# Low-rank factors split into 16-bit halves before the feed-forward weights are merged, in a perceiver block on one core

## The reference

```python
x = x + fake_quant(layernorm(x)) @ fake_quant(ctx)               # ctx: (16, 1024, 1024)
x = x + attention(layernorm(x), qkv_w, qkv_b, out_w, out_b)      # 32 heads of 32, rotary, causal
x = x + ffn(layernorm(x))
# ffn(h):  h @ W.T + bias + sum_e coeffs[e]*scales[e] * (h @ A[e].T) @ Bf[e].T     A: (16, 16, 1024)
```

## Time and profile before

| | us |
|---|---|
| median of 3 runs | 678.24 (678.01 to 678.92) |
| the profiled execution: its own time | 679.87 |
| its span (first to last record of the core) | 678.2 |
| TensorE's matmuls, busy | 619.1 (91%) |
| VectorE, busy | 457.4 (67%) |
| ScalarE, busy | 293.8 (43%) |

### The profile page before, as it was taken

The page is one execution under the profiler, slowest core; times in us unless marked ns, Lnnn a source line. Parts: engine busy times, 40 slices in busy tenths (PEclk is TensorE's granted clock), DMA queues, the critical chain, the costliest instruction groups (busy, mean ns, idle before and its releaser), DMA issues.

```text
span 678.2 us, 12785 instructions
## 1 busy us (share of the span) xinstructions
PE 619.1 (91%) x4848; PEld 311.2 (46%) x4848; DVE 457.4 (67%) x931; ACT 293.8 (43%) x370; POOL 7.6 (1%) x18
## 2 busy tenths in 40 slices
PE   0648967689999999999999999999999999799998
PEld 0223533345555554555555455555544544344453
DVE  8698984846854884586398558747754467675861
ACT  3986657256346346525643553555201233111010
POOL 1100000000000000000000000000000000000000
PEclk9869987879999999999999999999999999999999
DMA  8999864374157308514740761274300061032221
GB/s 321 388 387 401 303 257 155 104 254 147 58 186 242 130 17 295 182 62 146 249 162 0 275 220 62 103 268 154 125 31 1 1 238 75 1 108 95 92 83 57
DMA packets 38329, 109.09 MB, mean 161 GB/s; under 512 B 3994, under 2 KB 4250, under 8 KB 38304
## 3 DMA queue, kind: packets, MB, share of 16 engines
q1 hardware_dynamic: 36528, 104.35, 43.2%
q0 software_dynamic: 1344, 4.23, 1.6%
q10 hardware_dynamic: 432, 0.18, 0.1%
HBM read 100.35 MB, written 8.39 MB: 160 GB/s over the span
## 4 chain that ended last, share of the span: by engine, by line
PE 79%; DVE 14%; issue 3%; ACT 2%; DMA 1%; DVEq 0%; SPq 0%; ACTq 0%
PE dense L1032 14%; PE dense L1034 14%; PE dense L1033 14%; PE cross L1054 7%; PE turn L1022 6%; PE dense L1148 4%; PE cross L1174 4%; PE dense L1150 4%; PE dense L1149 4%; PE score L1109 3%; PE score L1135 2%; DVE wq L714 2%; PE dense L1041 1%; PE score L1098 1%; DVE nw L657 1%
## 5 line engine op out<-in xcount | busy, mean ns | idle before, releaser
L1032 PE MATMUL dense<-wq,xn_h 128*128 128x512 f16 x448 | 172.1, 384 | 5.1 <-DVE wq L782 2.3
L1033 PE MATMUL dense<-wq,xn_h 128*128 128x512 f16 x448 | 171.6, 383 | 0.0
L1034 PE MATMUL dense<-wq,xn_l 128*128 128x512 f16 x448 | 171.6, 383 | 0.0
L294 ACT ACTIVATE code<-raw,cst,qc 128x1024 uint8<-128x1024 f32 x77 | 94.4, 1238 | 16.8 <-DMA raw<-in_ctx 16.4
L1054 PE MATMUL cross<-code,q1t 128*128 128x512 f16 x256 | 76.0, 401 | 15.7 <-DVE xa L723 9.9
L1034 PEld LDWEIGHTS dense<-wq,xn_l 128*128 128x128 f16 x448 | 44.2, 99 | 54.2 <-issue 2.2
L1032 PEld LDWEIGHTS dense<-wq,xn_h 128*128 128x128 f16 x448 | 44.2, 99 | 53.7 <-issue 8.4
L1033 PEld LDWEIGHTS dense<-wq,xn_h 128*128 128x128 f16 x448 | 44.2, 99 | 46.4 <-issue 4.8
L745 DVE TENSOR_REDUCE smx<-score 128x8 f32<-128x512 f32 x32 | 21.9, 685 | 53.9 <-PE score L1109 53.9
L310 ACT ACTIVATE at<-turn 128x512 f32<-128x512 f32 x32 | 19.1, 596 | 87.1 <-PE turn L1022 87.1
L733 DVE TENSOR_TENSOR rope<-dense,cst 128x512 f32<-128x512 f32 x32 | 22.0, 688 | 49.4 <-PE dense L1034 49.4
(11 more groups left out here) (128 smaller groups left out, 852.6 us busy)
## 6 DMA issues: line engine op xcount, KB each, us to landing
raw<-in_ctx SPq DMA_DIRECT2D x77, 512.0 KB, 4.6
lnt<-in_ctx SPq DMA_DIRECT2D x35, 512.0 KB, 4.0
wq<-in_qkv_w SPq DMA_DIRECT2D x11, 512.0 KB, 13.4
wo<-in_qkv_w SPq DMA_DIRECT2D x10, 512.0 KB, 11.5
wo<-in_ctx SPq DMA_DIRECT2D x8, 512.0 KB, 8.6
wq<-in_ctx SPq DMA_DIRECT2D x8, 512.0 KB, 11.7
x_scratch<-xb SPq DMA_DIRECT2D x8, 512.0 KB, 3.0
wq<-x_scratch SPq DMA_DIRECT2D x8, 512.0 KB, 3.6
```

The source lines that it names most:

```text
L294: act.activation(low_bytes, src, ACT.Identity, scale=qc[:, 1:2], bias=z2).then_inc(s_u8, 1)
L1032: pe.matmul(bank[:, :], a_h[:, k, :], w_hi, start=(k == 0 and not started), stop=False)
L1033: pe.matmul(bank[:, :], a_h[:, k, :], w_lo, start=False, stop=False)
L1034: ins = pe.matmul(bank[:, :], a_l[:, k, :], w_hi, start=False, stop=(k == KC - 1))
```

## The change

The factors are no longer used as float32. SyncE loads each of the four pieces (128 x 1024: two of `A2`, two of `B2`) into a staging place of its own: the two halves of `raw`, `q1t`, and `lnt` after the last pair's `x_turn` (`s_xt`). ScalarE makes the high half of each (`lora_high`, times 64, and for `B2` times `w` too), VectorE the low half (`lora_low`). A merge is then six float16 matmuls, the same three terms as in `dense` for each of the two pieces of the rank. The product is 64 x 64 times too large, and `merged_sum` scales it back in the addition that it did already, now a `scalar_tensor_tensor`.

The loads of `W` move: units 0 to 3 into `raw` when two low halves are there (`s_llo` 2), units 4 and 5 into `lnt` when all four are, units 6 and 7 and then the right half after the last `qkv`. TensorE does merges 4 and 5 within `qkv` 5, after the second scores, merges 6 and 7 between the halves of `project`, 8 to 11 behind `y_turn(0)`, and 12 to 15 after rounds 0 to 3 of `ffn(0, 0, 0)`. `y_turn(1)` comes after round 4 instead of 3 of `ffn(0, 0, 1)`.

```diff
@@ views
-        la = code[:, 0:4, :].rearrange("p j d -> p (j d)").bitcast(F32).rearrange("p (j d) -> p j d", j=2)
-        lb = [q1v.bitcast(F32), code[:, 4:6, :].rearrange("p j d -> p (j d)").bitcast(F32)]
+        la = [[code[:, 2 * j + h, :] for h in range(2)] for j in range(2)]
+        lb = [[code[:, 4 + h, :] for h in range(2)], [code[:, 6 + h, :] for h in range(2)]]
+        lora_stage = [raw[:, 0, :], raw[:, 1, :], q1v.bitcast(F32), lnt[:, :]]
+        wt_lnt = lnt[:, :].rearrange("p (u n) -> p u n", u=2)
+        wt_load = {0: 0, 4: 1, 6: 2, 8: 3, 12: 4}
@@ ScalarE
+            def lora_high(n):
+                act.wait_ge(s_lora[n], 16)
+                if n == 0:
+                    act.wait_ge(s_cmm, CHUNKS * PAIRS)
+                if n == 2:
+                    act.wait_ge(s_lws, 1)
+                act.activation(lora_parts(n)[0], lora_stage[n], ACT.Copy,
+                               scale=WSC if n < 2 else lw[:, n - 2, 0:1]).then_inc(s_lhi, 1)
             def last_pair(i):
+                for n in range(4):
+                    lora_high(n)
                 qk_evac(i, 0)
@@ SyncE, after the last context load
-            load_quarter(0)
+            for j in range(2):
+                sp.dma_start(lora_stage[j], lora_a[j * P:(j + 1) * P, :]).then_inc(s_lora[j], 16)
+            sp.dma_start(lw[:, :, :], lora_w.rearrange("(j p) c -> p j c", p=P)).then_inc(s_lw, 16)
             sp.wait_ge(s_cmm, CHUNKS * PAIRS)
-            sp.dma_start(la, lora_a.rearrange("(j p) d -> p j d", p=P)).then_inc(s_ld2, 16)
-            for j in range(2):
-                sp.dma_start(lb[j], lora_b[j * P:(j + 1) * P, :]).then_inc(s_ld2, 16)
-            sp.dma_start(lw[:, :, :], lora_w.rearrange("(j p) c -> p j c", p=P)).then_inc(s_ld2, 16)
+            sp.dma_start(lora_stage[2], lora_b[0:P, :]).then_inc(s_lora[2], 16)
+            sp.wait_ge(s_xt, 2 * PAIRS)
+            sp.dma_start(lora_stage[3], lora_b[P:2 * P, :]).then_inc(s_lora[3], 16)
             store_x2(PAIRS - 2)
+            sp.wait_ge(s_llo, 2)
+            load_wt(0)
+            sp.wait_ge(s_llo, 4)
+            load_wt(1)
             sp.wait_ge(s_qkv, 6 * PAIRS)
-            load_quarter(1)
+            load_wt(2)
             sp.wait_ge(s_st, 32)
-            sp.dma_start(xs[0], x2_dram[0, :, :]).then_inc(s_x2[0], 16)
-            load_quarter(2)
-            sp.dma_start(xs[1], x2_dram[1, :, :]).then_inc(s_x2[1], 16)
-            load_quarter(3)
+            for n in range(2):
+                sp.dma_start(xs[n], x2_dram[n, :, :]).then_inc(s_x2[n], 16)
+            load_wt(3)
+            load_wt(4)
@@ VectorE
             def merged_sum(u):
                 dve.wait_ge(s_wf, u + 1)
-                dve.tensor_tensor(wt_unit(u), X[u % 2][:, :], wt_unit(u), ALU.add).then_inc(s_wsum, 1)
+                dve.scalar_tensor_tensor(wt_unit(u), X[u % 2][:, :], 1.0 / (WSC * WSC), wt_unit(u), ALU.mult, ALU.add).then_inc(s_wsum, 1)
-            def scale_factors():
-                dve.wait_ge(s_ld2, 64)
-                link(dve.tensor_tensor(lw[:, :, 0:1], lw[:, :, 0:1], lw[:, :, 1:2], ALU.mult))
-                for j in range(2):
-                    dve.tensor_scalar(lb[j], lb[j], lw[:, j, 0:1], None, ALU.mult).then_inc(s_lb, 1)
+            def lora_weights():
+                dve.wait_ge(s_lw, 16)
+                dve.scalar_tensor_tensor(lw[:, :, 0:1], lw[:, :, 0:1], WSC, lw[:, :, 1:2], ALU.mult, ALU.mult).then_inc(s_lws, 1)
+                dve.wait_ge(s_lws, 1)
+            def lora_low(n):
+                dve.wait_ge(s_lhi, n + 1)
+                hi, lo = lora_parts(n)
+                dve.scalar_tensor_tensor(lo, lora_stage[n], WSC if n < 2 else lw[:, n - 2, 0:1], hi, ALU.mult, ALU.subtract).then_inc(s_llo, 1)
             def last_pair(i):
-                scale_factors()
+                lora_weights()
+                for n in range(4):
+                    lora_low(n)
                 rotate(i, 0)
...
                 softmax_in(i, 2)
                 softmax_in(i, 3)
+                merged_sum(4)
                 softmax_out(i, 2)
                 softmax_out(i, 3)
+                merged_sum(5)
                 c_low(i, 0)
                 c_low(i, 1)
             def apply3(t, s):
                 if isinstance(t, int) and t == 0:
                     dve.wait_ge(s_xt, 2 * PAIRS)
+                    dve.wait_ge(s_wfl, 6)
@@ VectorE, after the last pair
-            stats3(0, 0)
-            apply3(0, 0)
             for u in range(4):
                 merged_low(u)
-            merged_sum(4)
-            merged_sum(5)
-            out_evac(PAIRS - 1, 0)
+            stats3(0, 0)
             merged_low(4)
             merged_low(5)
-            out_evac(PAIRS - 1, 1)
+            apply3(0, 0)
             merged_sum(6)
-            y_low(0, 0)
             merged_sum(7)
+            out_evac(PAIRS - 1, 0)
             merged_low(6)
             merged_low(7)
+            out_evac(PAIRS - 1, 1)
+            y_low(0, 0)
             merged_sum(8)
             merged(*range(9, 2 * KC))
@@ TensorE
             def merge(u):
                 if u == 0:
-                    pe.wait_ge(s_lb, 2)
+                    pe.wait_ge(s_llo, 4)
                     pe.wait_ge(s_ce, 4 * PAIRS)
                 if u >= 2:
                     pe.wait_ge(s_wsum, u - 1)
+                rank_rows = slice(k * P, (k + 1) * P)
                 for j in range(2):
-                    ins = pe.matmul(X[u % 2][:, :], la[:, j, k * P:(k + 1) * P], lb[j][:, cols],
-                                    start=(j == 0), stop=(j == 1))
+                    pe.matmul(X[u % 2][:, :], la[j][0][:, rank_rows], lb[j][0][:, cols], start=(j == 0), stop=False)
+                    pe.matmul(X[u % 2][:, :], la[j][0][:, rank_rows], lb[j][1][:, cols], start=False, stop=False)
+                    ins = pe.matmul(X[u % 2][:, :], la[j][1][:, rank_rows], lb[j][0][:, cols], start=False, stop=(j == 1))
                 ins.then_inc(s_wf, 1)
-                qkv(i, 5, {0: [at(scores, i, 1)], 1: [at(c, 10, 11)], 2: [at(c, 12, 13)], 3: [at(c, 14, 15), at(values_due, i, 0)], 4: [at(values, i, 0)],
+                qkv(i, 5, {0: [at(scores, i, 1)], 1: [at(c, 10, 11), at(m, 4)], 2: [at(c, 12, 13), at(m, 5)], 3: [at(c, 14, 15), at(values_due, i, 0)], 4: [at(values, i, 0)],
-                    merge(4)
-                    merge(5)
+                    merge(6)
+                    merge(7)
             y_turn(0)
-            for u in range(6, 12):
+            for u in range(8, 12):
                 merge(u)
-                between = {1 + 2 * k: [at(merge, 12 + k)] for k in range(4)} if first and n == 0 else {}
+                between = {k: [at(merge, 12 + k)] for k in range(4)} if first and n == 0 else {}
-                    between = {3: [at(y_turn, 1)]}
+                    between = {4: [at(y_turn, 1)]}
```

More of the change, by code:

```diff
@@ L196, in build @@
         s_st = sem("s_st")
-        s_ld2 = sem("s_ld2")
-        s_wt = [sem(f"s_wt{n}") for n in range(4)]
+        s_lora = [sem(f"s_lora{n}") for n in range(4)]
+        s_lw = sem("s_lw")
+        s_lws = sem("s_lws")
+        s_lhi = sem("s_lhi")
+        s_llo = sem("s_llo")
+        s_wt = [sem(f"s_wt{n}") for n in range(5)]
         s_fb = sem("s_fb")
-        s_lb = sem("s_lb")
         s_wf = sem("s_wf")
@@ L234, in wt_unit, with lora_parts @@
             k, cols = merge_unit(u)
-            return wt_early[:, u, :] if u < 4 else wt[:, k, cols]
+            if u < 4:
+                return wt_early[:, u, :]
+            return wt_lnt[:, u - 4, :] if u < 6 else wt[:, k, cols]
+        wt_load = {0: 0, 4: 1, 6: 2, 8: 3, 12: 4}
+        def lora_parts(n):
+            return la[n] if n < 2 else lb[n - 2]
         def staged(j):
@@ L573, in _, with load_wt @@
             wt_v = ffn_wt.rearrange("(k p) n -> p k n", p=P)
-            def load_quarter(n):
-                ks, cols = slice(4 * (n % 2), 4 * (n % 2) + 4), slice(n // 2 * NT, (n // 2 + 1) * NT)
-                sp.dma_start(wt_early if n == 0 else wt[:, ks, cols], wt_v[:, ks, cols]).then_inc(s_wt[n], 16)
-            load_quarter(0)
+            def load_wt(n):
+                ks = (slice(0, 4), slice(4, 6), slice(6, 8), slice(0, 4), slice(4, 8))[n]
+                cols = slice(0, NT) if n < 3 else slice(NT, DM)
+                sp.dma_start((wt_early, wt_lnt)[n] if n < 2 else wt[:, ks, cols], wt_v[:, ks, cols]).then_inc(s_wt[n], 16)
+            for j in range(2):
+                sp.dma_start(lora_stage[j], lora_a[j * P:(j + 1) * P, :]).then_inc(s_lora[j], 16)
+            sp.dma_start(lw[:, :, :], lora_w.rearrange("(j p) c -> p j c", p=P)).then_inc(s_lw, 16)
             sp.wait_ge(s_cmm, CHUNKS * PAIRS)
-            sp.dma_start(la, lora_a.rearrange("(j p) d -> p j d", p=P)).then_inc(s_ld2, 16)
-            for j in range(2):
-                sp.dma_start(lb[j], lora_b[j * P:(j + 1) * P, :]).then_inc(s_ld2, 16)
```

(24 more changed lines are left out.)

## The result

| | before | changed |
|---|---|---|
| median, us | 678.58 (678.01 to 678.96, 4 runs) | 672.02 (670.29 to 672.18, 4 runs) |
| ratio to before | | 0.9898, 95% interval 0.9880 to 0.9917 |
| profiled execution, us | 679.87, span 678.2 | 670.29, span 668.6 |

The changed kernel is faster by 6.9 us (0.0102 x 678.58; 5.6 to 8.1 by the interval), inside the forecast range of 668.0 to 673.2.

The account below looks back on a forecast made before the run. TensorE was taken as the bound (79% of the chain, VectorE 14%). Terms 6.7 + 1.05 + 2.6 - 2.7 = 7.65 us; with 7.6 off the shown median of 678.24, the forecast was 670.6 us, range 668.0 to 673.2.

Parts of the forecast that it names:

- a merge: On TensorE, six float16 matmuls at 0.216 us, 1.30 us instead of 1.72; 16 merges save 6.7 us.
- factors' split: Ahead of the last pair: rotation 0.3 us late, its consumer `qk_turn(7, 0)` unmoved; priced at 0, at most 1 us.
- wait before the values: TensorE's wait for VectorE's second subtraction in the last pair, filled by merges 4 and 5; 1.05 us gained.
- wait at merge 10: Behind `y_turn(0)`, TensorE stands for VectorE's sum 8; 2.7 us lost, bounds 0 and 3.7 us.
- end of merge 15: Last merge, which sets the next product's time through VectorE; ends at 578.2 against 585.8, 7.6 us sooner.
- next product: TensorE's product after `y_turn(1)`, set by merge 15's end; predicted near 588.9 against 596.56 before.
- The four rounds moved behind the last merge: Merges 12 to 15 after rounds 0 to 3 have four rounds less ahead of them; 2.6 us gained.
- the clock rival: TensorE's clock falls after the new stall; at most 2.9 us, giving 673.5, or 672.1 at half; chance 0.17.
- Less stall: No stall, or half of it, at merge 10; 669.3 to 667.9 us; chance 0.10.
- late VectorE: VectorE later than counted at `apply3(0)` or `c_low`, beyond 0.9 or 1.0 us of slack; about 672 us; chance 0.10.
- unchanged merges: Float16 merges no cheaper on TensorE; only 1.8 us gained, 676.4 us; chance 0.03.
- a blocked merge 0: Merge 0 waits for all four low halves and blocks product 1 of the last pair; slower; chance 0.02.

Follow-up runs that it names:

- mid_no_wait: Changed kernel with merges 4 to 7 all between the halves of the projection and VectorE's order of sum8_early; 0.9861 of the kernel before, stretch 88.19 us.
- high_first: Changed kernel with ScalarE's high halves 6 and 7 ahead of `y_high(0)` instead of behind it; 0.9858 of the kernel before, stretch 88.00 us.
- sum8_early: Changed kernel with VectorE's sums 8 and 9 ahead of low 6 and low 7 and the second output evacuation later; 0.9857 of the kernel before, stretch 86.98 us.
- late_rounds: Changed kernel with merges 12 to 15 back after rounds 1, 3, 5, 7 and `y_turn(1)` after round 3; 0.9927 of the kernel before, stretch 91.98 us.
- f16_old_order: Kernel before with only float16 factors and six-matmul merges, merges and VectorE essentially in the old order; 0.9911 of the kernel before, stretch 91.80 us.
- the second set: The changed kernel, unchanged, timed again against the kernel before; ratio 0.9891 (0.9874 to 0.9908), stretch 89.39 us.
- mid_merges: Changed kernel with merges 4 to 7 all between the halves of the projection, sums 4 and 5 between the first low halves; 0.9925 of the kernel before, stretch 92.30 us.
- longer_wait: Changed kernel with one more 128x1024 addition on VectorE just ahead of sum 8; 0.9926 of the kernel before, stretch 92.19 us.

## Why the prediction was right

The times below count from the start of the stretch, 499.36 before and 497.53 after, so that the early part of the trace stays out.

| step | predicted | measured |
|---|---|---|
| a merge | 1.30 us | 1.30 us |
| factors' split: `qk_turn(7, 0)` | 8.65, unmoved | 506.18 - 497.53 = 8.65 |
| wait before the values | gone, 1.05 | gone; 1.2 with its surroundings, by mid_no_wait |
| `y_turn(0)` | 62.3 | 62.23 |
| wait at merge 10 | 2.70 | 2.56 |
| end of merge 15 | 78.8 | 78.62 |
| `y_turn(1)` | 85.5 | 85.32 |
| next product | 89.5 | 89.39 |
| gain in the stretch | 7.65 | 7.81 |

**Each step.** What the steps add up to was right because the steps were, and not by errors that cancel: the largest is 0.2 us, at merge 15's end. The price of a merge came from rows of the same form and held: 0.216 us a matmul. The figure of the Trainium skill ("TensorE: Matmul & The Clock Gate", section "Back-to-back issue gap"), 131 ns, doesn't fit this stream either, as merges 8 and 9 show at 1.30 us for six. The split costs nothing although VectorE's rotation starts 5.46 us into the stretch (502.99) instead of 5.39: `qk_turn` waits for nothing. The new stall was mis-sized by 0.14 us only; its cause was the queue behind `y_high`, which high_first shows (1.39 us back when high 6 and 7 go ahead) and sum8_early shows from the other side (2.41 us back by order alone). The four rounds moved behind the last merge are worth 2.59 us in late_rounds, against the predicted 2.6.

**The terms weren't additive in one place.** The sum lists 6.7 us for the merges and 2.7 for the stall. f16_old_order shows that cheaper merges in the old order return 5.4, not 6.7: VectorE holds them back there too, by 1.3 us. The new order (merges 4 and 5 early, 12 to 15 early, VectorE's new sequence) adds 2.4 on top, of which 1.2 and 2.6 are gains, each measured in an order of its own, and the rest is paid by the longer wait at merge 10 (2.56 against 1.3 us).

**The whole time.** 670.6 was forecast and 672.02 measured, 1.4 us more. 0.3 of it is the median of the kernel before, which came out at 678.58 and not at 678.24. The change in the times is 6.9 us (or 7.4 in the second set) where the stretch gives 7.8. Both intervals, 5.6 to 8.1 and 6.2 to 8.6, hold 7.8, so there is nothing to explain that the times can tell. The span of 668.6 of the first profile flatters the kernel by the early clock, and the 679.87 us of before was above its median.

**The rivals.** The median of 672.02 is also what the clock rival forecast at half its price, 672.1, so the time alone doesn't tell the two apart; the traces do, for the executions that they show. The clock did not fall in three profiled executions of the changed kernel. It did in mid_merges, with the same 2.39 us of wait, and cost 1.69 us, near the low end of the 1.45 to 2.9 us that I had priced: the full price took 6 us at half clock, as behind 137.41, and here it was 3.4 us. So the rival exists, and the changed kernel stands close to it. Whether it happens in some of its timed executions is open. Less stall, late VectorE, unchanged merges and a blocked merge 0 did not occur. The factors were not late: VectorE went through all four low halves without idle time before 502.99.

## What to carry to other kernels

When one engine's work gets cheaper, write out the queue of the engine that feeds it, instruction by instruction, to the first result that it needs; here ten steps, each with a row of its own, gave the new wait to 0.14 us. The same list shows the remedy: an item that is ready (sum 8, high 6) stands behind one that waits, directly or through a third engine, for the very engine it would release. And compare two traces between two landmarks around the change before comparing spans; here 1.8 of 9.6 us were no part of it.

## What the runs showed of the hardware that I had not expected

- The granted clock fell to 0.50 behind a wait of 2.26 us of idle time in f16_old_order (resumed at 581.76), and not behind one of 2.26 us in the kernel before (588.22) or of 2.39 us in the changed one (565.78). The length of the wait alone doesn't decide at this size. Behind 3.52 us, in longer_wait, it fell too, but at a time at which it also fell behind 2.39 us.
- The fall has no fixed delay behind the wait. In longer_wait TensorE resumes at 568.45 at the full rate, and the clock is at 0.50 from 569.4 to 572.7; in late_rounds it is at 0.50 from 581.8, when TensorE resumes at 581.84. Each of the five falls behind such waits lasted 3.4 us and cost 1.7 us, or nothing.
- Where a wait for another engine follows within a few us, a slow clock costs nothing: late_rounds lost nothing to 3.4 us at 0.50, since `y_turn(1)` would have waited 1.5 us anyway.
